# Attention loop: the weighted sums of a step moved from the end of the step to directly behind its scores

## The reference, cut to what matters

```
mod = silu(c) @ wmod                     # six vectors for each of the 4 batches
h = layernorm(x) * (1 + ca) + sa         # x: 4 batches x 1024 tokens x 512
x = x + ga * attention(h)
h = layernorm(x) * (1 + cb) + sb
x = x + gb * moe(h)                      # a shared and 16 routed experts; untouched by the change
# attention(x), 16 heads of 32 numbers:
kqv = x @ Wqkv + bqkv                    # q, k, v of each head
scores = einsum(k, q) / sqrt(32)         # rows and columns of 1024 tokens
scores = triu(scores) + -10000 * tril(ones, -1)
out = einsum(softmax(scores), v) @ Wo + bo
```

## Time and profile before

| | before |
|---|---|
| median of 3 runs | 2240.82 us |
| the profiled execution | 2246.83 us |
| its span, first to last instruction | 2245.0 us |
| attention loop, first to last exponential | 130 to 1286 us of the span |
| PE busy | 1885.5 us, 84% |
| DVE busy | 1263.4 us, 56% |
| ACT busy | 821.8 us, 37% |
| POOL busy | 687.6 us, 31% |
| PE's granted clock, mean over the span | 0.92 of 2.4 GHz |

### The profile page before, as it was taken

The page is one execution under the profiler, slowest core; times in us unless marked ns, Lnnn a source line. Parts: engine busy times, 40 slices in busy tenths (PEclk is TensorE's granted clock), DMA queues, the critical chain, the costliest instruction groups (busy, mean ns, idle before and its releaser), DMA issues. The chain is left out here.

```text
span 2245.0 us, 35104 instructions
## 1 busy us (share of the span) xinstructions
PE 1885.5 (84%) x9947; PEld 1190.6 (53%) x9948; DVE 1263.4 (56%) x3069; ACT 821.8 (37%) x1372; POOL 687.6 (31%) x775
## 2 busy tenths in 40 slices
PE   4799988999889999898999867999999919999800
PEld 0555534655435555446555325777777718888700
DVE  3356666356565466673566537555555337575468
ACT  1335554255453255551455603222222104545400
POOL 0101115011133011160011245444444479060064
PEclk8789999899999899998999978999999959999955
DMA  6212232222404122312223051222222177554398
GB/s 214 69 41 52 51 85 68 57 57 57 114 1 115 24 56 57 100 55 68 57 57 72 5 188 61 92 94 87 93 89 85 61 236 252 172 186 150 132 330 299
DMA packets 108032, 232.38 MB, mean 104 GB/s; under 512 B 23512, under 2 KB 23512, under 8 KB 107884
## 3 DMA queue, kind: packets, MB, share of 16 engines
q1 hardware_dynamic: 84080, 171.87, 25.6%
q0 software_dynamic: 14848, 50.34, 6.4%
q10 hardware_dynamic: 8960, 8.41, 1.3%
HBM read 113.06 MB, written 67.17 MB: 80 GB/s over the span
## 5 line engine op out<-in xcount | busy, mean ns | idle before, releaser
L401 ACT ACTIVATE pr<-sc 128x1024 f32<-128x1024 f32 (+3 forms) x384 | 308.1, 811 | 264.7 <-PE sc L670 244.7
L325 POOL TENSOR_SCALAR_AFFINE_SELECT pr<-pr 128x256 f32<-128x256 f32 x256 | 105.7, 413 | 952.4 <-ACT pr L401 952.1
L690 PE MATMUL O<-pr,V 128*32 128x512 f32 (+3 forms) x3072 | 328.4, 501 | 14.5 <-ACT oD L413 14.5
L514 DVE TENSOR_REDUCE mx<-ring 128x1 f32<-128x512 f32 x256 | 169.6, 679 | 240.5 <-PE ring L645 238.9
L510 DVE CUSTOM_DVE_ANT_0 ring<-ring,mask 128x512 f32<-128x512 f32 (+3 forms) x512 | 240.9, 512 | 66.9 <-PE ring L645 64.7
L670 PE MATMUL sc<-stk 128*128 128x512 f32 (+3 forms) x768 | 244.6, 400 | 15.0 <-ACT pr L401 13.0
L670 PEld LDWEIGHTS sc<-stk 128*128 128x128 f32 x768 | 116.9, 191 | 255.3 <-ACT pr L401 153.0
L645 PE MATMUL ring<-stk 96*128 96x512 f32 (+3 forms) x768 | 216.2, 380 | 10.4 <-DVE mx L510 4.3
L645 PEld LDWEIGHTS ring<-stk 96*128 96x128 f32 x768 | 143.6, 201 | 57.6 <-DVE mx L510 19.1
L636 PE MATMUL ring<-hhi,whi 128*128 128x512 f32 x256 | 112.3, 439 | 26.6 <-DVE hlo L489 14.7
L539 DVE RECIPROCAL oD<-oD 128x128 f32<-128x128 f32 x128 | 117.7, 935 | 28.4 <-ACT oD L413 28.4
(11 more groups left out here) (246 smaller groups left out, 3779.0 us busy)
## 6 DMA issues: line engine op xcount, KB each, us to landing
stk<-st SPq DMA_DIRECT2D x384, 128.0 KB, 2.4
x_e<-xs SPq DMA_DIRECT2D x79, 256.0 KB, 2.6
ys<-y_e SPq DMA_DIRECT2D x79, 256.0 KB, 2.0
xt<-in_L_attn_x_dram ACTq DMA_DIRECT2D x16, 512.0 KB, 6.9
st<-in_L_attn_x_dram SPq DMA_DIRECT2D x32, 256.0 KB, 2.7
x1d<-pr SPq DMA_DIRECT2D x32, 256.0 KB, 2.0
xb<-x1d SPq DMA_DIRECT2D x32, 256.0 KB, 2.9
part<-y_sh SPq DMA_DIRECT2D x32, 256.0 KB, 2.0
```

The lines of the kernel that those rows point to most:

```text
L325: nc.gpsimd.affine_select(out=t, in_=t, compare_op=ALU.is_ge, fill=0.0, base=0, pattern=[[0, 2], [1, P]], channel_multiplier=-1).then_inc( ...
L401: nc.scalar.activation(pr[:, g % PRB, :, off:], sc[g % 2][:, :, off:], ACT.Exp, scale=SCALE).then_inc(exp_done, 1)
L514: nc.vector.tensor_reduce(mx[:, heads[0]:heads[-1] + 1, qt, part], bank[:, 0:len(heads) * w].rearrange("p (e k) -> p e k", e=len(heads)), ...
L690: last = nc.tensor.matmul(O[row:row + 32, off:], V[:, col:col + DH], pr[:, g % PRB, e, off:], start=(i == 0), stop=(i == 4 * c + 3))
```

## The change

The call of `weighted` moves from the end of PE's step to directly behind `scores`. Nothing is added or removed on any engine; ACT, DVE, POOL and SP keep their lists, and so does each wait.

```diff
                     for s in range(NST):
                         scores(b, p, s)
+                        g = p * NST + s - PV_LAG
+                        if g >= 0:
+                            weighted(b, g // NST, g % NST)
                         if p + 1 < NPAIR:
                             if s == 0:
                                 pe.wait_ge(stk_in[(p + 1) % NSLOT], stk_count(b, (p + 1) % NSLOT, p + 2))
...
                                 project(b, (p + 2) // 2, [P_AT.index(s)])
                             if s == MT_AT:
                                 m_transpose(b, p + 1)
-                        g = p * NST + s - PV_LAG
-                        if g >= 0:
-                            weighted(b, g // NST, g % NST)
```

## The result

The changed kernel takes 2286.23 us, the median of 4 runs (2283.05 to 2288.94), against 2242.17 us for the kernel before (4 runs, beside it). The ratio is 1.0194 with a 95% interval of 1.0177 to 1.0212: 44 us slower. The prediction said 2284 us, 43.5 us more.

A forecast was written before the change was run, and what follows sets the result against it. PE was taken to set the pace of a pair, waits included. Terms of 25.2 + 5.4 + 3.3 + 5.6 + 4.0 = 43.5 us on 2240.8 gave 2284 us, with 2260 to 2307 for 8 in 10.

The forecast's parts named there:

- ordinary steps, borders: Steps with the same instructions reordered: one entry to and one exit from the sums either way, 0, within 25 us.
- step 10, pairs 0 to 6: Sums wait 1.4 us for ACT's copies, transposes come behind instead of filling the wait: 0.9 us each, 25.2 us.
- step 2, pairs 1, 3 and 5: Two maxima no longer fill the wait for the copies: 9 x 0.6 and, at half clock, 3 x 1.1 us.
- step 2, pairs 2 and 4: The projection no longer covers the copy; PE waits 0.8 us, less 0.1 of a bank wait: 8 x 0.7 us.
- pair 6, beside step 10: DVE bounds steps 5 and 6; step 2's maxima reach it 1.9 us later: 4 x about 1.0 us.
- the three waits: PE's attention-loop waits: copies out of O (14.5 us), DVE freeing a ring bank, and before the transposes (12.8 us).
- The rival of better hidden weight loads: Maxima's weights load while sums stream, at most 0.25 us per step over 252 steps: 2221 us; chance 0.09.
- The copies end when ACT's list lets them: In steps 2 and 10, ACT's own list sets the copies out of O; having the sums earlier does not help.
- The rival that the copies were waiting for the sums: Earlier last sums of a half pull the copy ahead; step 10 loses 0.33 us, step 2 nothing: 2250 us; chance 0.06.
- The clock: Rival: longer gaps bring PE to 1.2 GHz, some 2.5 us in each of 28 pairs, 70 us more: 2354 us; chance 0.04.
- its own sign: The prediction counts as wrong if the clock is under 1.00 in pairs other than 0 and 5.
- The proof from pair 7: Argument against a lowered clock: pair 7 has gaps of 1.18 and 1.41 us and holds 1.00 throughout.

The follow-up runs named there:

- with S in time as well: The changed kernel with steps 2 (pairs 1 to 7), 8 and 10 in the old order: 2245.96 us, ratio 1.0000 to the kernel before.
- the best kernel: Against the kernel before: the new order only in step 2 of pair 0, ACT's copies out of O before the exponentials of steps 1 and 9; 2237.23 us, 0.9962.

## Why the prediction was right, and where it was not
The sum of the differences by steps, from the two traces, is 44.4 us in the loops. Term by term, forecast against measured:

| term of the prediction | forecast | measured |
|---|---|---|
| ordinary steps, borders | 0 | within 0.1 us a step, -0.7 in all |
| step 10, pairs 0 to 6 | 28 x 0.9 = 25.2 | 0.59 to 0.81 each, 19.8 |
| step 2, pairs 1, 3 and 5 | 5.4 + 3.3 | 9 x 0.41 + 3 x 0.4 = 4.9 |
| step 2, pairs 2 and 4 | 5.6 | 0.90 to 1.02 each, 7.5 |
| pair 6, beside step 10 | 4.0 | 4 x 1.1 = 4.4 |
| pair 7 | left out | 4 x 0.29 = 1.2 |
| pair 0, step 2 | 0 | -4.3 |
| pair 0, its start | 0 | -1.5 |
| the clock lowered in step 10 | 0 | 8 x 1.5 = 12 |
| step 11 | 0 | 1.3 |

- *PE sets the pace; in an ordinary step the borders cost nothing.* Right. Sums to maxima takes 0.99 us, as sums to scores did, and steps 3 and 5 (outside pair 5) and 9 are within 0.06 us. One reading was too strong: the three waits that were to account for almost all of PE's idle time in the loop come to 38 us in the earlier trace rows, of 59. Another 13.0 us are three waits for exponentials behind ACT's transfers in pair 5, which the prediction prices apart; no term changes by it. The rival of better hidden weight loads is refuted by the same rows: the sums did not get cheaper with maxima behind them.
- *The copies end when ACT's list lets them.* Right for the changed kernel, and shown by moving them: 40 us. The rival that the copies were waiting for the sums fell: in the changed kernel they start at 507.49, with the end of the exponentials (507.46), and the last sums are over at 506.97.
- *Step 10: the transposes were only hidden in that wait.* This step failed as a full account, though its price held. It took S as it was, with its 0.46 us of waiting "saved already counted", and looked at step 10 alone. The same edit also moves the last maxima of step 8 behind a sum and makes S 0.75 us later (2.62 us from the scores of step 9 to the transposes in the kernel with step 10 old, 1.87 before). In the changed kernel this stands in the shadow of the copies by 0.24 us in pair 1 (S ready at 508.57, the sums at 508.81) and by 0.10 us in pair 2, so the price came out near, 0.59 to 0.81 for 0.9. But undoing step 10 alone, which the working says would give back 25 us, gives next to nothing: 0.002 in the ratio, about 5 us, and less than the five slowed steps 10 that this execution had fewer. Two more kernels show it from both sides: with S in time as well steps 10 are back at 2.85 to 2.91 us, and with step 8 alone old they stay at 3.59 and 3.72.
- *The size of 0.9.* The transposes take 0.82 us to the scores (509.80 to 510.62), not 0.97; and in the even pairs the second copy comes 0.13 us sooner behind the exponentials (the gap is 1.27 us, against 1.40).
- *Step 2.* The mechanism is right. Two maxima behind the sums take 0.51 us, not 0.57, and 0.1 us is won by the borders. In pairs 2 and 4 the wait was 0.94 to 1.06 us, not 0.8. In pair 5 of the first three batches step 2 grew by 0.92 us, but steps 1 and 3, which lie in the same stretch at half clock, shrank by 0.5, so 0.4 us is left of the 1.1.
- *Pair 7.* Left out, since nothing of its own order changes. But ACT's four copies of the transposes now start late, behind a wait of 1.17 us for PE, and the exponentials of step 11 of pair 6 stand behind them; the prediction looked only at the scores of step 0, which were in time. The scores of step 1 of pair 7 wait for those exponentials (second batch):
```profile
670.79 0.73 PE L670 MATMUL sc<-stk 128*128 128x512 f32 x2 [0.26 <-ACT pr L401]
```
In the pairs before, maxima fill that place.
- *Pair 0.* Taken as unchanged in step 2, because its sums wait for no copy. They are the first of the batch, and placed between the maxima of steps 1 and 2 they cover the waits for the ring banks: 5.99 to 4.90 us in the second batch, and 1.08 to 1.09 us in every one. A term with the other sign, missed; the best kernel has about half of its gain from it. The 1.5 us in step 0 are no effect of the change: that step takes 5.8 to 7.3 us in the twelve traces, within one kernel too, because a part of it that differs from execution to execution runs at half clock.
- *The clock.* The rival had 0.04, with pair 7 against it, which has gaps of 1.18 and 1.41 us at 1.00. Eight of the 28 steps 10 did run at a lowered clock in the profiled run, two of each batch, and by its own sign (the clock under 1.00 in pairs other than 0 and 5) the prediction was wrong here, in pairs 2 and 3. Its size was less than the rival's (1.5 us each and not in all). The proof from pair 7 was a few gaps of a kind that is followed by a lowered clock in a part of cases only: pair 7 itself was slowed in step 10 in two other kernels and in step 2 in a third.

So the total was met within 0.1% with one cause understood halfway, one term of the other sign missed, and 12 us of clock that stood in for some 11 us by which the other terms were too large or missed. That is luck. One question stays open: which steps 10 are slowed (in the changed kernel pairs 2 and 5 in three batches and 3 and 5 in one, over all kernels pairs 1 to 6).

## What to carry to other kernels
When work is moved in an in-order list, list at each place both what now waits and what is now issued later, and follow the latter to its reader, even several steps on: the maxima of step 8 were due in step 10. A wait that has cover costs nothing until the cover moves; before undoing a move, look for a second thing in its shadow. Where a new order makes a buffer's last writer earlier, the copy that frees it must be moved ahead on its engine too, or the earlier end is not used. And an order mixed from two has borders of its own, which neither pure order shows.

## What the runs showed of the hardware that was not expected
Gaps of 1.18 to 1.41 us on PE are followed by 1.2 GHz in some places and not in others, in the same kernel. In steps 10 of pairs 0 to 6 that is eight of 28 in the changed kernel, three, four and seven with step 10, step 2 and both in the old order, one with step 8 old, and none where the gaps were 0.75 to 0.97 us (the gap filled in part, the copies first). A slowed step 10 takes 1.3 to 1.6 us more. In pair 7 four steps 10 and one step 2 were slowed, by 0.4 to 0.9 us, in the nine kernels in which their gaps are 1.33 to 1.41 and 1.18 us. Each kernel was profiled in one execution, so these counts are of one execution each.
